# Two-layer transformer block on one core: 4 KB fetches of attention rows, and work moved at both ends of the attention stage

## What is computed

```
x1 = _ln(x) * (scale1 + 1.0) + shift1
q, k, v = split(x1 @ mat_qkv_w.T + bias)          # 16 heads of 16 channels
q = _l2norm(q) * sm ; k = _l2norm(k)
probs = softmax(q @ k.T) ; o = probs @ v
x = x + (o @ proj_w.T + proj_b) * gamma1
x2 = _ln(x) * (scale2 + 1.0) + shift2
x = x + (gelu(x2 @ fc1_w.T + fc1_b) @ fc2_w.T + fc2_b) * gamma2
```

## Time and profile before

| what | value |
|---|---|
| median of three runs | 795.8 us (793.74 to 796.53) |
| the profiled execution | 793.83 us, its span 792.0 us |
| mean granted TensorE clock | 0.976 |
| PE busy | 731.9 us, 92% of the span |
| DVE, ACT, POOL busy | 498.2, 443.1, 326.1 us |
| packets, bytes moved by DMA | 83,096 packets, 79.65 MB, 71,710 of them under 2 KB |
| chain that ended last | PE 79%, ACT 6%, DVE 6%, issue 3% |

### The profile page before, as it was taken

How to read it: one execution, slowest core, us unless ns; L and a number is a source line. 1 busy time by engine, 2 the same in 40 slices (tenths; PEclk the granted TensorE clock), 3 DMA queues, 4 the chain that set the end, 5 groups by cost and what they waited for, 6 DMA issues and landing times.

```text
span 792.0 us, 15017 instructions
## 1 busy us (share of the span) xinstructions
PE 731.9 (92%) x4708; PEld 521.5 (66%) x4708; DVE 498.2 (63%) x1037; ACT 443.1 (56%) x733; POOL 326.1 (41%) x563
## 2 busy tenths in 40 slices
PE   4789999999996689999999999998889999999997
PEld 2477788888873345555555555555548888888885
DVE  2168999989999357767676767666425444444432
ACT  0335555555553266666666666666546555556553
POOL 1024655655653445555555555555442302222200
PEclk9999999999999599999999999999989999999999
DMA  8831333333311777776667767666500000000001
GB/s 239 292 98 37 111 94 115 115 94 113 103 32 40 126 133 149 148 147 150 146 147 146 147 147 147 146 147 155 125 14 1 22 19 14 27 27 28 14 27 40
DMA packets 83096, 79.65 MB, mean 101 GB/s; under 512 B 22942, under 2 KB 71710, under 8 KB 83054
## 3 DMA queue, kind: packets, MB, share of 16 engines
q1 hardware_dynamic: 81726, 78.95, 41.6%
q10 hardware_dynamic: 1328, 0.16, 0.1%
HBM read 57.13 MB, written 21.66 MB: 99 GB/s over the span
## 4 chain that ended last, share of the span: by engine, by line
PE 79%; ACT 6%; DVE 6%; issue 3%; DMA 1%; POOL 1%; ACTq 0%; SPq 0%; DVEq 0%; POOLq 0%
PE ps L1703 11%; PE ps L1717 11%; PE ps L1521 7%; PE ps L1439 7%; PE ps L1596 6%; PE ps L1582 6%; PE ps L1634 4%; PE ps L1531 4%; ACT probsT L928 4%; PE ps L1412 4%; PE ps L1430 4%; PE ps L1459 4%; PE ps L1470 3%; PE ps L1615 2%; PE ps L1548 1%
## 5 line engine op out<-in xcount | busy, mean ns | idle before, releaser
L928 ACT ACTIVATE probsT<-ps 128x1024 f32<-128x1024 f32 x128 | 130.5, 1019 | 29.8 <-PE ps L1582 29.5
L1331 DVE TENSOR_TENSOR hidden_low<-hidden,hidden_high 128x512 fp32r<-128x512 f32 x64 | 46.1, 721 | 115.0 <-ACT hidden_high L1024 67.1
L1021 ACT ACTIVATE hidden<-ps,b_fc 128x512 f32<-128x512 f32 x64 | 44.1, 689 | 73.5 <-PE ps L1703 72.5
L1582 PEld LDWEIGHTS ps<-q_stack,k_stack 49*128 49x128 f32 x512 | 39.0, 188 | 65.3 <-ACT probsT L928 35.3
L1582 PE MATMUL ps<-q_stack,k_stack 49*128 49x256 f32 x512 | 65.5, 335 | 11.9 <-ACT probsT L928 6.8
L1596 PE MATMUL ps<-probsT,v_ones 128*32 128x256 f32 x1024 | 69.2, 388 | 5.0 <-ACT probsT L928 4.8
L713 POOL TENSOR_TENSOR scores<-scores,row_max 128x640 f32<-128x640 f32 x32 | 42.4, 1324 | 76.2 <-DVE row_max L1060 76.2
L1225 DVE TENSOR_REDUCE neg_max<-ps 128x4 bf16<-128x344 f32 x128 | 59.5, 506 | 19.6 <-PE ps L1548 19.6
L1521 PE MATMUL ps<-w_qkv,x1T 128*128 128x512 f32 x128 | 65.3, 634 | 0.0
L1439 PE MATMUL ps<-x_res,w_q 128*128 (+1 forms) x256 | 63.7, 394 | 0.0
L1439 PEld LDWEIGHTS ps<-x_res,w_q 128*128 128x128 f32 x256 | 47.4, 194 | 11.1 <-issue 5.5
(11 more groups left out here) (181 smaller groups left out, 1714.2 us busy)
## 6 DMA issues: line engine op xcount, KB each, us to landing
parts_dram<-part_pairs SPq DMA_DIRECT2D x64, 256.0 KB
q_stack<-parts_dram SPq DMA_DIRECT2D x96, 128.0 KB, 5.3
k_stack<-parts_dram SPq DMA_DIRECT2D x96, 128.0 KB, 6.0
adj<-in_adj SPq DMA_DIRECT2D x16, 440.0 KB, 3.4
xT<-in_xT SPq DMA_DIRECT2D x16, 256.0 KB, 2.7
x_res<-in_x SPq DMA_DIRECT2D x16, 256.0 KB, 3.4
x_in<-in_x SPq DMA_DIRECT2D x16, 256.0 KB, 2.8
gate_rows<-rows_dram SPq DMA_DIRECT2D x16, 256.0 KB, 7.0
```

The costliest lines, as they stand in the source:

```text
L928: nc.scalar.activation(probsT[:, s % 4, :], ps[:, COLS:COLS + 2, :].rearrange("p a n -> p (a n)"), ACT.Exp).then_inc(exp_made, 1)
L1021: nc.scalar.activation(hidden[:, s % RAW, :], ps[:, FC1[s % FC1_BANKS], :], ACT.Gelu, bias=b_fc1[:, m:m + 1]).then_inc(gelu_made, 1)
L1331: nc.vector.tensor_tensor(hidden_parts[1][:, s % H_SLOTS, :], hidden[:, s % RAW, :], hidden_parts[0][:, s % H_SLOTS, :], ALU.subtract).the ...
L1582: mm = nc.tensor.matmul(ps[:, COLS + j, kt * N:(kt + 1) * N], k_stack[at, par, s, kt * P:(kt + 1) * P], q_stack[at, par, s, :], start=True ...
```

## The change

1. Channels inside each group of four heads are stored interleaved: channel `a*16 + d` (head a, channel d) goes to `d*4 + a`. DVE does it on the way: `take_qk` writes with a stride of 4 elements (16 bytes), `sum_squares` reads with that stride, and `unit_qk` reads and writes runs of 4. Four neighbouring partitions then hold one channel of four heads.
2. `parts_dram` gets the layout [part, channel row, token]. A store writes rows of 1 KB from 128 partitions (before 2 KB), and a fetch reads four neighbouring rows as one piece of 4 KB (before pieces of 1 KB). Bytes and DMA counts stay.
3. The mask `row_head` follows the layout; DVE makes it in the setup from the identity, not POOL.
4. `key_ones` is issued by ACT ahead of the turns, not by SP behind the first fetches.
5. In turn `f = 1`, DVE's `first_guess` (and `b_gated`) move from ahead of the turn to behind the first group of `maxima`.
6. `make_v` of batch 0 moves ahead of the turns, that of batch 15 from slot 2 to slot 0 (`take_v` from 3 to 1).
7. In turn `c = 14`: FFN statistics from slot 4 to 0, `ffn_normalise` from 8 to 4, `ffn_root` ahead of the split of w_fc1, `ffn_norm` into slot 7, `ffn_scale` into slots 8 and 9.
8. In turn `c = 15`: `first` in slots 2 and 5 (before 4 and 6), `project` in slot 6 (before 3), `gate` in 7 (before 4).

```diff
-    parts_dram = nc.dram_tensor("parts_dram", (2, HT, 2, HD, C2 * N), F32, kind="Internal").ap()
+    parts_dram = nc.dram_tensor("parts_dram", (2, 2, C2, P, N), F32, kind="Internal").ap()
...
-    FIRST_AT = (4, 6)
+    FIRST_AT = (2, 5)
...
+    def project_at(c):
+        return 6 if isinstance(c, int) and c == B - 1 else 5
+
+    def values_made_at(b):
+
+        return 0 if isinstance(b, int) and b == B - 1 else 2
...
+        def store(par, w, part):
+            return sp.dma_start(parts_dram[w, part].rearrange("c p n -> p c n"), parts[:, par, w, part].bitcast(F32).rearrange("p (c n) -> p c n", c=C2))
...
-                sp.dma_start(parts_dram[w, :, 0], parts[:, par, w, 0].bitcast(F32)).then_inc(parts_out, 16)
+                store(par, w, 0).then_inc(parts_out, 16)
...
-                sp.dma_start(stack[at:at + SLOT, par].bitcast(F32), parts_dram[w, :, part, :, c * N:(c + 1) * N].rearrange("h d n -> d h n")
+                sp.dma_start(stack[at:at + SLOT, par].bitcast(F32).rearrange("d (j a) n -> d j (a n)", j=2),
+                             parts_dram[w, part, c].rearrange("(j d a) n -> d j (a n)", j=2, d=HD)
                              ).then_inc(stack_in, 16)
...
             if isinstance(c, int) and c == B - 2:
+                ffn_root(0)
                 pool.wait_ge(g["late_weights"], g["LATE"])
...
-                if isinstance(c, int) and c == B - 1 and s < C2:
-                    ffn_scale(0, (s,))
+                if isinstance(c, int) and c == B - 2 and s >= SLOTS - C2:
+                    act.wait_ge(s_mm, GROUPS * B)
+                    ffn_scale(0, (s - (SLOTS - C2),))
...
+        act.wait_ge(x_made, B)
+        for c in range(C2):
+            at = HALF * c + KROWS
+            act.dma_start(k_stack[at:at + 1].bitcast(F32).rearrange("o a h n -> o (a h n)").rearrange("o (p e) -> o p e", p=P),
+                          ones_r[:]).then_inc(key_ones_in, 16)
...
-            nc.vector.tensor_tensor(qk[:, tt, :], ps[:, qk_bank(f, tt), :], bias_qk[:], ALU.add).then_inc(qk_out, 1)
+            by_head = "p (g a d) -> p g a d"
+            nc.vector.tensor_tensor(qk[:, tt, :].rearrange("p (g d a) -> p g a d", d=HD, a=4), ps[:, qk_bank(f, tt), :].rearrange(by_head, d=HD, a=4),
+                                    bias_qk[:].rearrange(by_head, d=HD, a=4), ALU.add).then_inc(qk_out, 1)
...
-            nc.vector.tensor_reduce(sum_sq[:, tt * 2 * H:(tt + 1) * 2 * H], squares[:, tt].rearrange("p (h d) -> p h d", d=HD), AX_X,
+            nc.vector.tensor_reduce(sum_sq[:, tt * 2 * H:(tt + 1) * 2 * H], squares[:, tt].rearrange("p (g d a) -> p g a d", d=HD, a=4), AX_X,
...
+                if isinstance(f, int) and f == 1 and s == 1:
+                    first_guess(f)
...
-                if b is not None and s == 2:
+                if b is not None and s == values_made_at(b) and not (isinstance(b, int) and b == 0):
                     make_v(b, 1 - par)
...
+                if isinstance(c, int) and c == B - 2 and s == 7:
+                    ffn_norm(0)
...
+        pe.wait_ge(qk_out, FRONT * T)
+        make_v(0, 0)
         turns(turn, pe, 4, first=1, last=B + 2)
```

More of the change, by code:

```diff
@@ L290, in _ @@
                     nc.vector.memset(v_blocks[:], 0.0).then_inc(v_zeroed, 1)
+                    dve.wait_ge(consts_set, 5)
+                    nc.vector.tensor_reduce(row_head[:], ident[:].rearrange("p (q a) -> p a q", a=HT // 2), AX_X, ALU.add).then_inc(row_heads, 1)
+                    dve.wait_ge(row_heads, 1)
+                    nc.vector.tensor_scalar(row_head[:], row_head[:], 1.0 / 3.0, None, ALU.mult).then_inc(row_heads, 1)
                     dve.wait_ge(small_in, 10 * 16)
@@ L636, in put_low @@
                 sp.wait_ge(rest_made, 2 * n + w + 1)
-                sp.dma_start(parts_dram[w, :, 1], parts[:, par, w, 1].bitcast(F32)).then_inc(low_out, 16)
+                store(par, w, 1).then_inc(low_out, 16)
         def fetch(stack, par, slot, w, part):
@@ L676, in turn @@
                 get_low(b, 1 - par)
-                if isinstance(b, int) and b == 0:
-                    key_ones()
                 max_row(b, 1 - par)
@@ L956, in turn @@
                     square(f, s - 1)
-                if b is not None and s == 3:
+                if b is not None and s == values_made_at(b) + 1:
                     take_v(b, 1 - par)
@@ L1214, in unit_qk @@
             ge(dve, qkt_mm, 2 * f)
[L1215 to L1216 removed]
+            rows = "p t (g d a) -> p (t g) d a"
+            nc.vector.tensor_tensor(qkn[:].rearrange(rows, d=HD, a=4), qk[:].rearrange(rows, d=HD, a=4),
+                                    root[0][:].rearrange("p (g a) -> p g a", a=4).unsqueeze(2).broadcast_to([P, HH // 4, HD, 4]), ALU.mult).then_inc(qkn_made, 1)
         def maxima(b, n):
@@ L1266, in turn @@
                     maxima(b, n)
+                if isinstance(f, int) and f == 1 and s == 1:
+                    first_guess(f)
+                    for k in range(C2):
+                        nc.vector.tensor_scalar(b_gated[:, k, :], ada[:, k, :], b_proj[:, k:k + 1], None, ALU.mult).then_inc(gated_bias, 1)
                 if ahead is not None and s == 0:
@@ L1282, in turn @@
                     divide(d)
-                if d is not None and s == back_at(c) + 3:
+                if d is not None and s == project_at(c) + 1:
                     gate(d)
@@ L1370, in _ @@
         sum_squares(1, 1)
-        first_guess(1)
         dve.wait_ge(x_made, B)
-        for k in range(C2):
-            nc.vector.tensor_scalar(b_gated[:, k, :], ada[:, k, :], b_proj[:, k:k + 1], None, ALU.mult).then_inc(gated_bias, 1)
         turns(turn, dve, 4, first=1, last=B + 2)
@@ L1647, in turn @@
             for s in range(SLOTS):
-                if isinstance(c, int) and c == B - 1 and s == 0:
-                    ffn_norm(0)
                 if c is not None and s < 8:
@@ L1664, in turn @@
                     output_channels(d, f)
-                if d is not None and s == back_at(c) + 2:
+                if d is not None and s == project_at(c):
                     project(d)
```

22 lines of the change are left out of this document (4 added, 18 removed).

## The result

The changed kernel takes 800.83 us (median of 4 runs, 800.11 to 801.85), the kernel before 795.12 (4 runs). The ratio is 1.0067, with a 95% interval from 1.0044 to 1.0091: **slower by 5.7 us**, where 9.8 us less were forecast. The profiled execution of the change took 801.85 us, with a span of 800.1 at a mean clock of 0.976.

What follows compares the result with a forecast made beforehand. PE, busy 731.9 us, was taken to bound the kernel, with idle time at both ends. Start 5.7 plus end 4.1 gave 9.8 us off 795.8, so 786.0 us; own range 782.5 to 790.7, with rivals 781 to 798.5.

Steps and rivals of the forecast that it cites:

- I take 0: Steady turns: DVE's new access patterns in `take_qk`, `sum_squares` and `unit_qk` add no time at the same number of elements.
- my two bounds: Steady turns: the new stride adds between nothing and 0.53 us to each `take_qk` and `sum_squares`.
- the stride costs: Rival, steady turns: DVE's chain from `take_qk` to `unit_qk` grows 1.4 us a turn, 19.6 us, giving 805.6 us; chance 0.15.
- 5.7 us forecast: Start of the turns: first column scores move from 272.9 to 267.2 us; bounds 3.6 to 7.3 us.
- My 267.2 us: Start: time of PE's first column scores, after first fetch at 255.2 and last bytes at 266.1 us.
- The bound of 3.6 without quicker stores: Start: lower bound of the gain, 3.6 us, if the stores do not get quicker.
- The store's gain of 1.8 us: Start: 1.8 us off the 6.0 us between first store's issue and first fetch; bounds 0 and 3.
- No gain in the rate: Start: twelve fetches stay at 153 GB/s despite 4 KB pieces, 10.3 us for 1.57 MB; other bound 5.6 us.
- The pieces were the limit: Rival, start: PE binds at 265.6 us, start gains 7.3 and end 6 us, giving 782.5 us; chance 0.08.
- 4.1 us forecast: End, last two turns: 2.15 us less PE idle plus 1.9 us of low-clock excess; bounds 1.5 and 6 us.
- the clock's part: End: two thirds of the 2.90 us low-clock excess in v of batch 15 and the last projection, 1.9 us.
- a steady turn over 20 us: Sign that the forecast is wrong, read from the steady turns, forecast at 19.7 us.

Runs made afterwards that it cites:

- The probe: Kernel before plus 26 DVE instructions on 512 elements of idle tiles in the setup, at steps of 4 to 32 bytes; run once for its trace, 812.2 us.
- The layout alone: Kernel before with heads interleaved by four, 4 KB fetches and stores by rows, none of the schedule changes: 805.7 us, ratio 1.0140.
- the moves alone: Kernel before with the schedule changes at start and end, heads in rows, old stores and 1 KB fetches: 790.4 and 789.7 us in two sets.
- the twos: Changed kernel with heads interleaved by two in place of four, so an 8-byte step and 2 KB fetches: 790.7 us, ratio 0.9951.
- the step in `sum_squares` alone: Changed kernel with query and key weight columns and bias permuted on the host, so `take_qk` has no step: 793.0 us, ratio 0.9974.
- the end moves: Kernel before with only the schedule changes at the end (v of batch 15, last projection, FFN statistics sooner): 790.3 us, ratio 0.9948.

## Why the prediction was wrong

**Steady turns: the step that failed.** "I take 0, as these instructions already run at one 4-byte element per 1.04 ns and not at a packed rate." That says only that these instructions do not run at a packed rate; it says nothing of what a step costs. The probe has 0.38 us for 512 elements. It lies between my two bounds, nothing and 0.53, nearer to the second. The rival "the stride costs" was the true case; its 1.4 us a turn were too much, the turns measured 0.79. (With 0.38 in its own sum it would have been 0.95.) Its path was only half right. I looked at DVE's chain to `split_qk`, and did not look at ACT's `square`, behind which the exponentials queue. Over the 13 turns 0.79 us are 10.3. The layout alone measured +11.1, with the gain of its stores already taken off.

**Start: 5.7 us forecast, about 1.1 for the moves by their runs.** My 267.2 us came from a model, the 272.9 it was taken from out of the trace. Put through the same steps, the kernel before gives 257.0 + 0.6 + 10.3 + 1.1 = 269.0 us, not 272.9. So 3.9 of the 5.7 us were the error of the model, and 1.8 the stores. (The bound of 3.6 without quicker stores should by the same steps have been 3.9.) Two of its terms were short, by 2.1 us together; the other 1.8 are not broken down. The 153 GB/s of the earlier trace rows contain the last bytes of the stores; the fetches alone ran at 137 in that execution (262 to 269 us), 11.5 us in place of 10.3. And from the last bytes to PE it is about 2 us, not 1.1. The single times were good: the first guess at 256.25 us and `unit_qk` at 262.19 in the run with the moves alone (256.3 and 262.2 forecast). The store's gain of 1.8 us measured 2.6 (from the first store's issue to the first fetch, 6.0 to 3.4 us), inside its bounds.

**"No gain in the rate" of the fetches: right by the trace.** The change's fetches ran at 138 GB/s, the kernel before's at 137:

```profile
262.00:269.00 7.00, 3.89 (x17) 2.00 (x18) 4.92 (x12) 2.07 (x4) 4.05 (x13) 0.50 1.06 138
```

Behind the same wide store, pieces of 1 KB ran at 122 and 116, of 2 KB at 130, of 4 KB at 138, 133 and 131. So 1 KB is a little slower there; between 2 and 4 KB these traces tell nothing. "The pieces were the limit" is refuted all the same; 4 KB gave no start under 17.6 us.

**End: 4.1 us forecast, 4.1 measured** with its moves alone (2.6 to 5.6), 3.4 in the trace of the change. The clock fell once, at 567.5 to 574.5 us (granted 0.51, the low one of its two levels), in place of twice (555.5 to 559.5 and 576 to 583 us before).

How often it falls is not set by the list alone. The moves alone had one fall of 3.5 us in one trace and none in the other. I count from the last `split_qk` to the last column scores:

| falls of the clock | with the end's moves | without |
|---|---|---|
| none | 36.7, 37.2, 37.5 us | |
| one of about 3.5 us | 38.4 | |
| one of about 7 us | 39.0, 39.4 (the change) | 41.5 |
| both | 40.0, 40.2, 40.2 | 42.3, 42.9 (before) |

At equal falls the order of the work gives 2.1 to 2.9 us, and the falls that come or stay away are worth up to 3.5 us. The forecast had 2.15 us for the order and 1.9 for the clock. The first held in the traces; that the clock's part came out so close in the medians is partly luck.

**The sum.** The moves were worth 5.3 us (the end's 4.1 and 1.1 at the start) and the layout cost 11.1: 795.8 - 5.3 + 11.1 = 801.6 us, beside 800.8. The range, 781 to 798.5, left out the case that came, to which I gave 0.15. The text's own test, "a steady turn over 20 us", was the one that spoke.

## What to carry to other kernels

- When a change gives an instruction an access pattern that no row of the trace has, its price is a cost to measure or to carry in the middle of the range, not one to set to zero because "the elements are the same". Here a step of 8 bytes is free for 512 elements of 4 bytes and one of 16 bytes adds 0.38 us to 0.69, so this layout could be had in twos where fours cost.
- Put the kernel before through your own model before you take a difference from a measured time. What the model misses there is otherwise booked as a gain.
- For an instruction that gets longer, follow everything that waits for it, on each engine's queue, also what merely stands behind the waiting one.

## What the runs showed that was not expected

- ACT's `square`, writing 4-byte elements 64 bytes apart, took 1.07 us for 512 in place of 0.63.
- The stores' form changed what follows: behind the stores with 128 rows outermost, 1 KB fetches ran at 122 and 116 GB/s, against 136 to 157 in five executions with the old stores, and the page's median landing of a `k_stack` fetch went from 6.0 to 8.0 and 7.5 us (7.3 with 4 KB). Part of the wide store's gain was so paid back before the first columns. Nothing here says why.
- The traces differ by up to 6 us at 69 us already (66.8 to 72.9), ahead of all that these kernels change in the turns; the one kernel with two traces had 67.2 and 66.8. The granted clock parts them. The latest six had 0.50 from 36 to 42 us (the twos and both kernels with 1 KB fetches behind wide stores; 0.76 to 0.78 in the others) or 0.83 from 60 to 70 us (the change, the step in `sum_squares` alone, the end moves, the twos; 1.00 in the others). The twos had both and came last. What sets it off is not shown. A difference of that size between two single traces says nothing, unless it is counted from a landmark nearby.
